# Graph attention with layer norm: one score tile in forty-eight goes from VectorE to ScalarE and GpSimd

## The chip, the cores and the metric

The kernel runs on one core of a Trainium2 chip. The metric is the device time of one execution in microseconds (us); times below are medians over runs on the chip. The core has five engines with a queue of instructions each: TensorE (PE in the profile; its weight loads stand apart as PEld), VectorE (DVE), ScalarE (ACT), GpSimd (POOL) and SyncE (SP, which here only issues transfers). An engine works its queue strictly in order; engines meet at semaphores, written by hand in this kernel.

## The reference

For each of 16 batches: 512 nodes with 384 features, 12 heads of 32 features, a boolean adjacency of 512 x 512 per batch.

```
h    = einsum('bnd,ade->bane', x, W);  th = tanh(h)
attn = (th @ w_src) + (th @ w_dst)^T;  attn = where(attn >= 0, attn, 0.2 * attn)
attn = softmax(where(adj, attn, -999))
o    = elu(attn @ h + b)                      # heads put side by side
gate = sigmoid(x @ H_w.T + H_b)
out  = layernorm(x + gate * o + (1 - gate) * x)
```

## The kernel before

The kernel has B = 16 steps, numbered b, each of which works on one batch and prepares the next. In a step the attention is done in HP = 6 pairs of heads, j = 0 to 5, each pair over C = 4 row blocks (c) of 128 nodes, so that a batch has 4 * H = 48 **score tiles** `ew` of 128 x 512 fp32 in the order t = 8j + 2c + k. The exponential of a leaky ReLU of a sum is split into factors, so that a tile is max(v, u) * adj: `v_all` is a row vector of the head, spread over all partitions by a transfer through memory; `u` is a scalar per partition; `ADJ` is the adjacency, turned into words that lie in PSUM (banks `adj01` and `adj23`). VectorE makes a tile in one instruction (`edges`, L820), TensorE multiplies it with `vals` (`attend`, L1082, two passes per tile), ScalarE copies the result out (`copy_out`, L525), TensorE turns it back (`transpose_out`, L1090) and VectorE divides by the sum (`attended`, L829 and L834). `ew` has SLOTS = 16 buffers; `ew_ready` counts the tiles made and `ew_free` those consumed.

Every order is written out by hand and is the same in each of the steps b = 1 to 13. What the prediction's steps touch:

- ScalarE (`step`): the copy of head pair 3, `gates(b, 2)` (L480), four row sums (L560), `gates(b, 3)`, four splits of x for batch b + 2 (L463), four small `out_bias` copies (L515), two row squares (L567), the adjacency words of blocks 0 and 1 of the next batch (`adjacency`, L505), `copy_out` 4, two more squares, adjacency blocks 2 and 3, `copy_out` 5; then step b + 1 begins with `features`, the tanh of the next batch's first block (L471).
- GpSimd: `weigh` (L296, then the half sums L302) for the four blocks, a bias transfer, `subtract_x` and `mix` (L339, L344, L347), `add_rows`, `values` (L333), `mean`, `split_low` (L307), a transfer, `variance` and `scale` (L355 to L364).
- VectorE: 48 tiles and between them, at fixed places, the rest: in j = 0 the divisions of the batch before, after the first tile of j = 1 the first `head_sums` (L782, waits for GpSimd's half sums), and so on until `scores_max` (L786) behind the last tile of j = 2. At tiles 0 and 4 of j = 0 it waits for two and four adjacency copies (`adj_done`).
- TensorE: features of the next batch (L982), heads 0 and 1, gates 0 and 1, `max_T` (L1014, waits for `scores_max`), heads 2 and 3, gates 2 and 3, heads 4 and 5, and the next features.

Of the kernel before, what the change touches and what calls it, by code (L numbers as in the profile page):

```python
# [6 lines left out]
BF16 = mybir.dt.bfloat16  # L7
# [3 lines left out]
ALU = mybir.AluOpType  # L11
# [3 lines left out]
P = 128  # L15
# [6 lines left out]
def gat_layernorm(nc, x, xT, adjT, W, HwT, w_rows, bias, H_b, out):  # L22
# [22 lines left out]
    VSLOTS = 3  # L45
    VB = 32
    assert N == 512 and H * E == D and B % 2 == 0

    ctx = ExitStack()
    with ctx:  # L50
# [6 lines left out]
        def sem(name):  # L57
# [6 lines left out]
        x_in = sb("x_in", [P, C, D])  # L64
        adj_in = sb("adj_in", [P, C, N], U8)

        w_hi = sb("w_hi", [P, KD, 2 * D], F32R)
# [32 lines left out]
        v_all = sb("v_all", [P, VSLOTS, 2, N])  # L100
        u = sb("u", [P, 2, C, H])
        vals = sb("vals", [P, 2, C, H, VW])
        gate_tanh = sb("gate_tanh", [P, C, D])
# [47 lines left out]
            scores mxT_done mxb_done exps_done v_turned vals_done  # L151
            ew_ready ew_free outT_copied tr_done inv_done att_done
            out_bias_done x_forms_done gate1_done elu_exp_done elu_done mixed moments sums_done mean_done squares_done var_done rstd_done y_done ld_x_last rest_last_done exp_last_done elu_last_done y_early_done elu_late_done y_late_done stats_done last_y_done""".split()
# [39 lines left out]
        def _(sp):  # L193
# [33 lines left out]
            def step(b, q, first, last, ahead=True):  # L227
# [11 lines left out]
                for j in range(VSLOTS, HP):  # L239
                    sp.wait_ge(S["ew_ready"], 4 * H * b + 2 * C * (j - 2))  # L240
                    load_v(b, q, j)
# [7 lines left out]
                if not last:  # L249
                    store_v(b + 1, 1 - q)  # L250
                    sp.wait_ge(S["st_v"], 64 * b + 128)
                    for j in range(VSLOTS):
                        if j:
                            sp.wait_ge(S["ew_ready"], 4 * H * b + 2 * C * (j + 4))
                        load_v(b + 1, 1 - q, j)
# [11 lines left out]
        def _(pool):  # L267
# [57 lines left out]
            def values(b, q):  # L325
# [3 lines left out]
                for c in range(C):  # L329
                    if isinstance(b, int) and b == 0:  # L330
# [3 lines left out]
                                    o[:, :, E:E + 1].broadcast_to([P, H, E]), ALU.mult).then_inc(S["vals_done"], 1)  # L334

            def subtract_x(b):
                pool.wait_ge(S["elu_done"], b + 1)
                pool.wait_ge(S["x_forms_done"], b + 1)
                g.tensor_tensor(ex[:], ex[:], x_plus1[:], ALU.subtract).then_inc(S["mixed"], 1)  # L339
# [26 lines left out]
            def step_last(b, q):  # L366
# [6 lines left out]
                pool.wait_ge(S["rest_last_done"], 1)  # L373
                g.tensor_tensor(rest_last[:], x_last, rest_last[:], ALU.subtract).then_inc(S["rest_last_done"], 1)
                y = y_last[:, :, EARLY]
                pool.wait_ge(S["exp_last_done"], 3)
# [9 lines left out]
            def step(b, q, first, last, ahead=True):  # L386
# [14 lines left out]
                if not last:  # L401
                    add_rows(b + 1, 1 - q)
                    values(b + 1, 1 - q)
                if not first:
                    mean(b - 1)
# [22 lines left out]
        def _(act):  # L428
            a = nc.scalar

            def before():
# [9 lines left out]
                for c in range(C):  # L441
                    adjacency(0, c)
                act.wait_ge(S["dve_setup"], DVE_SETUP)
                exps(0, 0)
# [43 lines left out]
            def exps(b, q):  # L488
# [10 lines left out]
                a.activation(vals[:, q, :, :, E], s_pos[:], ACT.Copy, scale=LIFT).then_inc(S["exps_done"], 1)  # L499

            def adjacency(b, c):
                act.wait_ge(S["ld_adj"], 16 * b + 16)
                if not isinstance(b, int) or b:
                    act.wait_ge(S["ew_ready"], 4 * H * b - 2 * C + 4 * (c // 2) + 4)
                a.activation(ADJ_WORDS[c // 2][:, c % 2], adj_in[:, c].bitcast(U16), ACT.Copy).then_inc(S["adj_done"], 1)  # L505

            def out_biases(b, q):
# [72 lines left out]
            def step(b, q, first, last, ahead=True):  # L580
# [24 lines left out]
                copy_out(b, q, 3)  # L605
                gates(b, 2)
                row_sums(b - 1)
                gates(b, 3)
# [7 lines left out]
                copy_out(b, q, 4)  # L616
                row_squares(b - 1, 2, C)
                for c in range(2, C):
                    adjacency(b + 1, c)
                copy_out(b, q, 5)  # L620

            def step_first(b, q):
# [11 lines left out]
                copy_out(b, q, 3)  # L634
                gates(b, 3)
                for c in range(C):
                    split(b + 2, q, c)
                copy_out(b, q, 4)
                for c in range(2):
                    adjacency(b + 1, c)  # L640
                out_biases(b + 1, 1 - q)
                for c in range(2, C):
                    adjacency(b + 1, c)
                copy_out(b, q, 5)

            def step_last(b, q):
# [13 lines left out]
                row_sums(b - 1)  # L660
                copy_out(b, q, 3)
                exp_early(q)
                copy_out(b, q, 4)
# [40 lines left out]
        def _(dve):  # L704
# [98 lines left out]
            def edges(b, q, j, between):  # L803

                for i in range(2 * C + 1):
                    for f in between.get(i, ()):
                        f()
                    if i == 2 * C:
                        break
                    c, k = i // 2, i % 2  # L810
                    h = 2 * j + k
# [130 lines left out]
        def _(pe):  # L942
# [125 lines left out]
            def attend(b, q, j):  # L1068
# [5 lines left out]
                for c in range(C):  # L1074
                    if j == 0 and isinstance(b, int) and b == 0:
                        pe.wait_ge(S["vals_done"], c + 1)
                    for k in range(2):
                        h = 2 * j + k
                        t = 2 * C * j + 2 * c + k

                        pe.wait_ge(S["ew_ready"], 4 * H * b + t + 1)
                        te.matmul(OUT[j % 2][VW * k:VW * k + VW, :], vals[:, q, c, h, :], ew[:, t % SLOTS, :],  # L1082
                                  start=(c == 0), stop=(c == C - 1)).then_inc(S["ew_free"], 1)
# [128 lines left out]
```

## Time and profile before

| | |
|---|---|
| time, median of 3 runs | 658.76 us (658.52 to 658.85) |
| the profiled execution | 658.69 us, its span 656.9 us |
| TensorE busy | 630.9 us (96%) |
| VectorE busy | 639.0 us (97%) |
| ScalarE busy | 429.6 us (65%) |
| GpSimd busy | 571.4 us (87%) |
| score tiles on VectorE | 768, 522.7 us together, mean 727 ns |
| chain that ended last | TensorE 48%, VectorE 30%, GpSimd 7%, ScalarE 2% |

The mean of one instruction is longer than the distance from one to the next, since neighbours on an engine overlap a little: 768 tiles of 727 ns would be 558 us, and take 522.7 us.

### The profile page before, as it was taken

The page shows a single profiled execution, that of the slowest core. Times are in us where ns is not written, and L with a number is a line of the kernel's source. Part 1 is how long each engine was busy: PE and PEld are TensorE (multiplying, and loading weights), DVE is VectorE, ACT ScalarE, POOL GpSimd, SP SyncE. Part 2 cuts the span into 40 slices and gives each one's busy share as a digit, 9 for nine tenths or more (in the row PEclk, how much of TensorE's full clock was granted, in tenths as well). Part 3 has the DMA queues.
Part 4 walks back from the last instruction along what each step waited for, and adds up shares of the span by engine and source line. Part 5 has one row for each costly group of instructions (what it writes and reads, how often), then busy time and mean ns, then how long its engine had stood idle before and what let it go on. Part 6 is the DMA issues. An engine that isn't in the chain of part 4 may idle for free.

```text
span 656.9 us, 12491 instructions
## 1 busy us (share of the span) xinstructions
PE 630.9 (96%) x3279; PEld 373.0 (57%) x3279; DVE 639.0 (97%) x1174; ACT 429.6 (65%) x936; POOL 571.4 (87%) x448
## 2 busy tenths in 40 slices
PE   8999999999999999999999999999999999999983
PEld 5565656574565647556664665656456565745531
DVE  7999999999999999999999999999999999999996
ACT  5434658486784848768485775848578584866664
POOL 2576998989989998998989999898999989997293
PEclk9999999999999999999999999999999999999997
DMA  6356549578475856848586584857747585675602
GB/s 209 118 131 181 178 123 274 128 196 248 140 235 129 235 164 176 240 146 251 133 210 190 154 238 144 249 132 200 228 142 233 139 259 126 187 211 131 217 40 97
DMA packets 54747, 117.62 MB, mean 179 GB/s; under 512 B 7106, under 2 KB 32452, under 8 KB 54724
## 3 DMA queue, kind: packets, MB, share of 16 engines
q1 hardware_dynamic: 42196, 81.56, 38.5%
q0 software_dynamic: 4320, 23.59, 19.2%
q10 hardware_dynamic: 8208, 12.19, 4.9%
q8 instruction: 11, 0.18, 0.1%
q14 instruction: 12, 0.10, 0.0%
HBM read 104.35 MB, written 12.98 MB: 179 GB/s over the span
## 4 chain that ended last, share of the span: by engine, by line
PE 48%; DVE 30%; issue 8%; POOL 7%; DMA 2%; ACT 2%; DVEq 1%; SPq 0%; POOLq 0%; ACTq 0%
PE out_T L1082 30%; DVE ew L820 20%; PE hg L982 13%; POOL th_w L296 4%; DVE sd L782 4%; DVE ex L842 3%; PE tr L1090 2%; POOL th_w L302 2%; PE hg L1047 1%; ACT th L471 1%; DMA xT_in<-in_xT 1%; DVE att L834 1%; DVEq L819 1%; PE hg L1014 1%; PE hg L1018 1%
## 5 line engine op out<-in xcount | busy, mean ns | idle before, releaser
L820 DVE SCALAR_TENSOR_TENSOR ew<-v_all,u,adj 128x512 f32<-128x512 f32 x768 | 522.7, 727 | 1.9 <-DMA v_all<-v_rows 1.2
L1082 PE MATMUL out_T<-ew,vals 128*64 128x512 f32 x1536 | 346.9, 597 | 0.0
L1082 PEld LDWEIGHTS out_T<-ew,vals 128*64 128x64 f32 x1536 | 106.3, 136 | 188.8 <-issue 144.1
L525 ACT ACTIVATE att_T<-out_T,out_bias 128x512 f32<-128x512 f32 x96 | 65.9, 686 | 116.1 <-PE out_T L1082 115.6
L296 POOL TENSOR_TENSOR th_w<-th,score_w 128x768 f32<-128x768 f32 x60 | 110.6, 1844 | 24.3 <-ACT th L471 24.3
L982 PE MATMUL hg<-w_hi,xT_hi 128*128 128x384 f32 x384 | 96.9, 360 | 0.8 <-ACT xT_hi L463 0.8
L982 PE MATMUL hg<-w_lo,xT_hi 128*128 128x384 f32 x384 | 88.2, 337 | 0.0
L982 PE MATMUL hg<-w_hi,xT_lo 128*128 128x384 f32 x384 | 87.7, 336 | 0.0
L302 POOL TENSOR_TENSOR th_w<-th_w 128x384 f32<-128x384 f32 x60 | 82.6, 1376 | 4.7
L982 PEld LDWEIGHTS hg<-w_hi,xT_hi 128*128 128x128 f32 x384 | 62.6, 189 | 40.2 <-issue 39.4
L982 PEld LDWEIGHTS hg<-w_lo,xT_hi 128*128 128x128 f32 x384 | 69.1, 188 | 0.0
L982 PEld LDWEIGHTS hg<-w_hi,xT_lo 128*128 128x128 f32 x384 | 68.9, 188 | 0.0
L333 POOL TENSOR_TENSOR vals<-h_sb,vals 128x384 f32<-128x384 f32 x64 | 53.3, 866 | 16.2 <-ACT vals L499 16.2
L339 POOL TENSOR_TENSOR ex<-ex,x_plus 128x1536 f32<-128x1536 f32 x15 | 56.4, 3758 | 11.4 <-ACT x_plus L530 11.4
L307 POOL TENSOR_TENSOR xT_lo<-xT_in,xT_hi 128x384 fp32r<-128x384 f32 x60 | 58.6, 1014 | 0.5 <-ACT xT_hi L463 0.5
L1090 PE MATMUL tr<-ident,att_T 128*128 128x128 f32 x384 | 53.1, 273 | 4.8 <-ACT att_T L525 4.8
L347 POOL TENSOR_TENSOR y<-x_in,ex 128x1536 f32<-128x1536 f32 x15 | 52.1, 3470 | 2.2 <-POOL ex L344 2.0
L344 POOL TENSOR_TENSOR ex<-gate,ex 128x1536 f32<-128x1536 f32 x15 | 52.0, 3467 | 1.4
L480 ACT ACTIVATE gate_tanh<-hg 128x384 f32<-128x384 f32 x60 | 29.5, 492 | 34.1 <-PE hg L982 32.8
L1090 PEld LDWEIGHTS tr<-ident,att_T 128*128 128x128 f32 x384 | 45.6, 141 | 10.8 <-ACT att_T L525 8.7
L471 ACT ACTIVATE th<-hg 128x384 f32<-128x384 f32 x64 | 31.7, 495 | 29.6 <-PE hg L982 29.6
L782 DVE TENSOR_REDUCE sd<-th_w 128x24 f32<-128x384 f32 (+1 forms) x64 | 36.5, 570 | 3.9 <-POOL th_w L302 3.7
(116 smaller groups left out, 669.0 us busy)
## 6 DMA issues: line engine op xcount, KB each, us to landing
v_all<-v_rows SPq DMA_DIRECT2D x95, 512.0 KB, 4.6
xT_in<-in_xT SPq DMA_DIRECT2D x16, 768.0 KB, 9.5
h_sb<-in_bias POOLq DMA_DIRECT2D x15, 768.0 KB, 6.7
x_in<-in_x SPq DMA_DIRECT2D x15, 768.0 KB, 4.6
gate_tanh<-in_H_b POOLq DMA_DIRECT2D x15, 768.0 KB, 9.4
out<-y ACTq DMA_DIRECT2D x15, 768.0 KB, 3.7
adj_in<-in_adjT SPq DMA_DIRECT2D x16, 256.0 KB, 9.8
v_rows<-v_turn SPq DMA_DIRECT2D x64, 6.0 KB
```

Of the source, the lines that this page charges most:

```text
L296: g.tensor_tensor(th_w[:, c % 2], th[:, c].unsqueeze(1).broadcast_to([P, 2, D]), score_w[:], ALU.mult).then_inc(S["thw_done"], 1)
L302: g.tensor_tensor(t[:, :, 0:E // 2], t[:, :, 0:E // 2], t[:, :, E // 2:E], ALU.add).then_inc(S["thh_done"], 1)
L307: g.tensor_tensor(xT_lo[:, q, :, n], xT_in[:, :, n], xT_hi[:, q, :, n].bitcast(F32), ALU.subtract).then_inc(S["xlo_done"], 1)
L333: g.tensor_tensor(o[:, :, 0:E], h_sb[:, c].rearrange("p (h e) -> p h e", e=E), o[:, :, E:E + 1].broadcast_to([P, H, E]), ALU.mult).then_in ...
L339: g.tensor_tensor(ex[:], ex[:], x_plus1[:], ALU.subtract).then_inc(S["mixed"], 1)
L347: g.tensor_tensor(y[:], x_in[:], ex[:], ALU.add).then_inc(S["mixed"], 1)
L525: a.activation(att_T[:, j % 2], OUT[j % 2][:], ACT.Identity, bias=out_bias[:, q, j:j + 1]).then_inc(S["outT_copied"], 1)
L782: ve.tensor_reduce(sd_ckh[:, 2 * H * c:2 * H * (c + 1)], t, AX.X, ALU.add).then_inc(S["sd_done"], 1)
L820: ve.scalar_tensor_tensor(out=twos(ew[:, (2 * C * j + i) % SLOTS, :]), in0=twos(v_all[:, j % VSLOTS, k]), scalar=u[:, q, c, h:h + 1], in1= ...
L982: last = te.matmul(o, l, r, start=(i == 0), stop=(i == len(mms) - 1))
L1082: te.matmul(OUT[j % 2][VW * k:VW * k + VW, :], vals[:, q, c, h, :], ew[:, t % SLOTS, :], start=(c == 0), stop=(c == C - 1)).then_inc(S["ew ...
L1090: last = te.transpose(TR[j % 2][:, c * P:(c + 1) * P], att_T[:, j % 2, c * P:(c + 1) * P], ident[:])
```

## The change

The last tile of each batch, t = 47 (head 11, row block 3), is no longer made by VectorE. ScalarE makes max(v, u) in two passes, relu(v - u) and then + u, after a small instruction that negates `u`; GpSimd multiplies the result with `adj_side`, a bf16 copy of the adjacency's last row block that ScalarE makes once per batch from `adj_in`. `ew_ready` counts 47 tiles per batch (EW), TensorE waits for `side_ready` ahead of tile 47, and the third `v_all` load of the next batch also waits for ScalarE's passes.

```diff
+    SIDE = 1
+    EW = 4 * H - SIDE
+        adj_side = sb("adj_side", [P, N], BF16)
+        minus_u = sb("minus_u", [P, SIDE])
...
 SyncE
-                            sp.wait_ge(S["ew_ready"], 4 * H * b + 2 * C * (j + 4))
+                            sp.wait_ge(S["ew_ready"], EW * b + min(2 * C * (j + 4), EW))
+                        if j == VSLOTS - 1:
+                            sp.wait_ge(S["side_scored"], 2 * SIDE * b + 2 * SIDE)
                         load_v(b + 1, 1 - q, j)
...
 GpSimd
+            def side_tiles(b):
+                pool.wait_ge(S["adj_side_done"], b + 1)
+                pool.wait_ge(S["side_scored"], 2 * SIDE * b + 2 * SIDE)
+                tiles = ew[:, SLOTS - SIDE:SLOTS, :]
+                g.tensor_tensor(tiles, tiles, adj_side[:].unsqueeze(1).broadcast_to([P, SIDE, N]), ALU.mult).then_inc(S["side_ready"], 1)
...
                     values(b + 1, 1 - q)
+                side_tiles(b)
                 if not first:
                     mean(b - 1)
...
 ScalarE
+            def side_tiles(b, q):
+                act.wait_ge(S["side_ready"], b)
+                for i in range(SIDE):
+                    h = H - SIDE + i
+                    a.activation(minus_u[:, i:i + 1], u[:, q, C - 1, h:h + 1], ACT.Copy, scale=-1.0).then_inc(S["side_u"], 1)
+                act.wait_ge(ld_v[2], 32 * b + 32)
+                act.wait_ge(S["ew_free"], 4 * H * b + 4 * H)
+                act.wait_ge(S["side_u"], SIDE * b + SIDE)
+                for i in range(SIDE):
+                    k = 2 - SIDE + i
+                    a.activation(ew[:, SLOTS - SIDE + i, :], v_all[:, 2, k], ACT.Relu, bias=minus_u[:, i:i + 1]).then_inc(S["side_scored"], 1)
+                for i in range(SIDE):
+                    h = H - SIDE + i
+                    act.wait_ge(S["side_scored"], 2 * SIDE * b + i + 1)
+                    a.activation(ew[:, SLOTS - SIDE + i, :], ew[:, SLOTS - SIDE + i, :], ACT.Identity,
+                                 bias=u[:, q, C - 1, h:h + 1]).then_inc(S["side_scored"], 1)
...
-                    act.wait_ge(S["ew_ready"], 4 * H * b - 2 * C + 4 * (c // 2) + 4)
+                    act.wait_ge(S["ew_ready"], EW * b + (0 if c // 2 else SIDE - C))
...
+            def adjacency_side(b):
+                if not isinstance(b, int) or b:
+                    act.wait_ge(S["side_ready"], b)
+                a.activation(adj_side[:], adj_in[:, C - 1], ACT.Copy).then_inc(S["adj_side_done"], 1)
...
                 gates(b, 2)
+                side_tiles(b, q)
                 row_sums(b - 1)
...
                 row_squares(b - 1, 2, C)
+                adjacency_side(b + 1)
                 for c in range(2, C):
                     adjacency(b + 1, c)
...
 VectorE
+                    if 2 * C * j + i >= EW:
+                        continue
...
 TensorE
-                        pe.wait_ge(S["ew_ready"], 4 * H * b + t + 1)
+                        if t < EW:
+                            pe.wait_ge(S["ew_ready"], EW * b + t + 1)
+                        elif t == EW:
+                            pe.wait_ge(S["side_ready"], b + 1)
```

In step b = 0 `side_tiles` stands behind `gates(b, 3)`, in the last step behind `copy_out` 3, and GpSimd's in the last step behind the second `rest_last`.

ScalarE's queue in a middle step, from the gate copy of block 2 to the row sums. Before:

```order
L480 ACTIVATE gate_tanh<-hg 128x384
L554 REGISTER_ALU
L556 REGISTER_ALU
L560 ACTIVATE scratch,sums<-y 128x384 x2
L559 REGISTER_ALU
L560 ACTIVATE scratch,sums<-y 128x384
```

Of the change, where three instructions (a 128x1 negation and two passes over a tile) stand ahead of the row sums:

```order
L495 ACTIVATE gate_tanh<-hg 128x384
L520 ACTIVATE minus_u<-u 128x1
L521 ISA
L526 ACTIVATE ew<-v_all,minus_u 128x512
L529 ISA
L530 ACTIVATE ew<-ew,u 128x512
L591 REGISTER_ALU
L593 REGISTER_ALU
L597 ACTIVATE scratch,sums<-y 128x384 x2
```

So all that follows in this queue, the four adjacency copies too, stands behind three instructions more.

The same queue from the first adjacency copies to the next step's first tanh. Before:

```order
L505 ACTIVATE adj<-adj_in 128x256 x2
L519 REGISTER_ALU
L522 REGISTER_ALU
L525 ACTIVATE att_T<-out_T,out_bias 128x512
L567 ACTIVATE scratch,squares<-y,neg_mean 128x384 x2
L505 ACTIVATE adj<-adj_in 128x256 x2
L519 REGISTER_ALU
L522 REGISTER_ALU
L525 ACTIVATE att_T<-out_T,out_bias 128x512
L466 ISA
L471 ACTIVATE th<-hg 128x384
```

Of the change:

```order
L537 ACTIVATE adj<-adj_in 128x256 x2
L556 REGISTER_ALU
L559 REGISTER_ALU
L562 ACTIVATE att_T<-out_T,out_bias 128x512
L604 ACTIVATE scratch,squares<-y,neg_mean 128x384 x2
L542 ACTIVATE adj_side<-adj_in 128x512
L537 ACTIVATE adj<-adj_in 128x256 x2
L556 REGISTER_ALU
L559 REGISTER_ALU
L562 ACTIVATE att_T<-out_T,out_bias 128x512
L481 ISA
L486 ACTIVATE th<-hg 128x384
```

The copy of `adj_side` stands ahead of the adjacency blocks 2 and 3 and so also ahead of `copy_out` 5 and the tanh.

GpSimd's queue between `values` and `split_low` of a middle step, of the change:

```order
L339 TENSOR_TENSOR vals<-h_sb,vals 128x12x32 x4
L344 ISA
L346 TENSOR_TENSOR ew<-ew,adj_side 128x512
L362 ISA
L363 TENSOR_TENSOR neg_mean<-sums,minus_share 128x4
```

The multiply stands between what were neighbours; it is the one instruction that this queue gains.

## Rows read from the trace of the kernel before

**Rows 1.** Windows, six turns from 195 to 428 us: busy us of each engine

```profile
sum 233.00, PE 229.53 PEld 137.28 DVE 230.85 ACT 160.48 POOL 220.19; mean PE 38.26 PEld 22.88 DVE 38.47 ACT 26.75 POOL 36.70
```
**Rows 2.** Chain in order of time, 273 to 352 us: start us, us, what

```profile
277.20 0.33 PE hg L1014
...
315.94 0.33 PE hg L1014
...
328.54 7.02 PE out_T L1082 x32
335.55 1.80 PE hg L982 x9
...
338.12 1.86 POOL th_w L296
...
340.06 1.03 POOL th_w L302
...
341.11 0.05 DVE sd L782
```
**Rows 3.** Timeline of VectorE, 311 to 350 us: start us, us, what [idle before]

```profile
328.57 9.37 DVE L820 SCALAR_TENSOR_TENSOR ew<-v_all,u,adj 128x512 f32<-128x512 f32 x14
...
341.11 0.55 DVE L782 TENSOR_REDUCE sd<-th_w 128x24 f32<-128x384 f32 x1 [0.40 <-POOL th_w L302]
...
342.90 1.75 DVE L842 SCALAR_TENSOR_TENSOR ex<-ex,att 128x1536 f32<-128x1536 f32 x1
```
**Rows 4.** Timeline of ScalarE, 311 to 352 us

```profile
332.01 0.67 ACT L505 ACTIVATE adj<-adj_in 128x256 int32<-128x256 uint16 x2
...
334.49 0.67 ACT L505 ACTIVATE adj<-adj_in 128x256 int32<-128x256 uint16 x2
335.70 0.69 ACT L525 ACTIVATE att_T<-out_T,out_bias 128x512 f32<-128x512 f32 x1 [0.54 <-PE out_T L1082]
337.47 0.49 ACT L471 ACTIVATE th<-hg 128x384 f32<-128x384 f32 x1 [1.07 <-PE hg L982]
```
**Rows 5.** Window of one stretch: busy us (x instructions) by engine, clock, DMA, GB/s

```profile
325.95:335.70 9.75, 9.75 (x53) 4.93 (x51) 9.75 (x18) 9.09 (x31) 9.59 (x14) 1.00 0.67 203
```
**Rows 6.** Timeline of GpSimd, 311 to 352 us

```profile
330.12 0.22 POOL L351 TENSOR_TENSOR neg_mean<-sums,minus_share 128x4 f32<-128x4 f32 x1
...
336.64 0.20 POOL L364 TENSOR_TENSOR shift<-neg_mean,rstd 128x4 f32<-128x4 f32 x1
338.12 1.86 POOL L296 TENSOR_TENSOR th_w<-th,score_w 128x768 f32<-128x768 f32 x1 [1.28 <-ACT th L471]
...
342.98 2.54 POOL L302 TENSOR_TENSOR th_w<-th_w 128x384 f32<-128x384 f32 x1
```
**Rows 7.** Groups by line and form: busy us, mean ns of one | idle before

```profile
L525 ACT ACTIVATE att_T<-out_T,out_bias 128x512 f32<-128x512 f32 x96 | 65.9, 686 | 116.1 <-PE out_T L1082 115.6
...
L307 POOL TENSOR_TENSOR xT_lo<-xT_in,xT_hi 128x384 fp32r<-128x384 f32 x60 | 58.6, 1014 | 0.5 <-ACT xT_hi L463 0.5
...
L567 ACT ACTIVATE scratch<-y,neg_mean 128x384 f32<-128x384 f32 x60 | 36.2, 605 | 1.3 <-POOL neg_mean L351 1.0
...
L463 ACT ACTIVATE xT_hi<-xT_in 128x384 fp32r<-128x384 f32 x64 | 28.1, 513 | 0.8 <-DMA xT_in<-in_xT 0.8
L319 POOL TENSOR_TENSOR hb_sum<-h_sb 128x768 f32<-128x768 f32 x15 | 27.7, 1847 | 4.7 <-DMA h_sb<-in_bias 4.7
...
L495 ACT ACTIVATE u<-d_rel 128x48 f32<-128x48 f32 x16 | 3.6, 227 | 0.0
```
**Rows 8.** Timeline of GpSimd in step b = 0

```profile
68.09 1.02 POOL L302 TENSOR_TENSOR th_w<-th_w 128x384 f32<-128x384 f32 x1
```
**Rows 9.** Timeline of VectorE in step b = 0

```profile
69.30 0.53 DVE L782 TENSOR_REDUCE sd<-th_w 128x24 f32<-128x384 f32 x1
```
**Rows 10.** Timeline of VectorE in the last step, its first and last tiles

```profile
605.72 4.04 DVE L820 SCALAR_TENSOR_TENSOR ew<-v_all,u,adj 128x512 f32<-128x512 f32 x6 [0.20 <-DMA v_all<-v_rows]
...
643.91 0.69 DVE L896 SCALAR_TENSOR_TENSOR ex<-ex,att 128x512 f32<-128x512 f32 x1 [0.21 <-ACT ex L686]
```

More of the change, by code:

```diff
@@ L151, in gat_layernorm @@
             scores mxT_done mxb_done exps_done v_turned vals_done
-            ew_ready ew_free outT_copied tr_done inv_done att_done
+            ew_ready ew_free adj_side_done side_u side_scored side_ready outT_copied tr_done inv_done att_done
             out_bias_done x_forms_done gate1_done elu_exp_done elu_done mixed moments sums_done mean_done squares_done var_done rstd_done y_done ld_x_last rest_last_done exp_last_done elu_last_done y_early_done elu_late_done y_late_done stats_done last_y_done""".split()
@@ L239, in step @@
                 for j in range(VSLOTS, HP):
-                    sp.wait_ge(S["ew_ready"], 4 * H * b + 2 * C * (j - 2))
+                    sp.wait_ge(S["ew_ready"], EW * b + 2 * C * (j - 2))
                     load_v(b, q, j)
@@ L403, in step @@
                     values(b + 1, 1 - q)
+                side_tiles(b)
                 if not first:
@@ L442, in before @@
                     adjacency(0, c)
+                adjacency_side(0)
                 act.wait_ge(S["dve_setup"], DVE_SETUP)
@@ L635, in step_first @@
                 gates(b, 3)
+                side_tiles(b, q)
                 for c in range(C):
@@ L641, in step_first @@
                 out_biases(b + 1, 1 - q)
+                adjacency_side(b + 1)
                 for c in range(2, C):
@@ L661, in step_last @@
                 copy_out(b, q, 3)
+                side_tiles(b, q)
                 exp_early(q)
```

## The prediction

> **What bounds the kernel now.** The table of busy shares comes first and settles nothing: in six turns of the middle (233 us) VectorE is busy for 230.85 us and TensorE for 229.53 us [rows 1]. Both look full, so the question is which of them waits for what, and the chain in order of time answers it. It repeats with a period of 38.74 us, from one `max_T` (277.20) to the next (315.94) [rows 2]. In one turn it runs:
>
> 1. TensorE from `max_T` at 315.94 through heads 2 to 5 and the gates to the end of the next batch's first features, 335.55 + 1.80 = 337.35 [rows 2]: 21.4 us without a gap.
> 2. ScalarE's tanh of these features at 337.47 [rows 4], GpSimd's product at 338.12 and its half sums, 340.06 to 341.09 [rows 2]: 3.8 us.
> 3. VectorE's first `head_sums` at 341.11 [rows 2], then everything in its queue up to `scores_max`, for which the next `max_T` waits: the remaining 13.6 us (38.74 - 25.17).
>
> The reader is to see what part 3 does not hold. Tile 47 stands ahead of it. VectorE's 14 tiles from 328.57 are eight of j = 5 and six of the next j = 0, one every 0.663 us ((9.37 - 0.07) / 14, the last one's tail taken off) [rows 3]; so tile 47 is made from 333.2 to 333.87, and at 341.11 VectorE has already stood 0.40 us for GpSimd's half sums [rows 3]. This small wait is the place that decides: the tile taken out lies on the side of it that is early.
>
> **What the change removes.** 0.66 us of VectorE per batch, ahead of that wait. In the middle of the kernel the 0.40 us would only become 1.06 us: worth nothing. The next batch's `v_all` transfer also comes just in time there; at the first tile of the last step VectorE waits 0.20 us for it [rows 10], so the tile gone there is worth nothing either. In step b = 0 VectorE runs without waits, and its first `head_sums` at 69.30 follows half sums that end at 68.09 + 1.02 = 69.11 [rows 8, 9]: worth 0.2 us once. At the end the tile stands ahead of an instruction that waits 0.21 us for ScalarE's exponential [rows 10]: nothing.
>
> **What it adds on ScalarE, first block.** At 325.95, behind the gate copy, come the negation and two passes. No row is 512 wide with SBUF on both sides; the nearest are `copy_out` with 686 ns (512 wide, but from PSUM) and the squares with 605 ns (SBUF and the same kind of bias, but 384 wide) [rows 7]. The squares' 605 and the 0.08 us from them to `copy_out` say that a pass is at least 0.69; I take a little more, 0.71 us, because SBUF is read. The negation is a small instruction like the `u` exponential, 0.23 us [rows 7]. Each waits for the one before it, so neighbours do not overlap, except the last by 0.1 us: 0.23 + 0.71 + 0.71 + 0.1 for three hand-overs - 0.1 = **1.65 us**. Bounds: 0.605 a pass, as if the width cost nothing, gives 1.4; the squares widened in proportion, 605 x 512 / 384 = 0.81, and hand-overs twice as long give 2.0.
>
> The Trainium skill ("ScalarE: Activation LUTs", What ACT_TABLE_LOAD costs) gives 280 ns + 0.833 ns per element with a pointer bias, 186 ns without, and an overlap of about 93 ns between neighbours. For these three that is 0.19 + 0.71 + 0.71 - 0.09 = 1.5 us, an estimate; 605 ns at 384 wide [rows 7] fits it (600). By it each turn would lose 0.15 us less than by my sum, 2 us in all.
>
> **Second block.** The `adj_side` copy, 512 wide without a pointer bias, has 513 ns at 384 wide beside it [rows 7]: 0.62 us, and 0.52 us as a distance to the next. Bounds 0.33 (a word copy, 0.67 for two [rows 4]) and 0.7.
>
> Is there room for 2.17 us? From 325.95 to 335.70 ScalarE is busy for 9.09 of 9.75 us [rows 5], nearly all of the rest being the 0.54 us before `copy_out` 5, and before the tanh it has 1.07 us more [rows 4]. With the 0.1 us of overlap that each idle stretch also cost, the room is 1.8 us. What is late next, path by path:
>
> - *The tanh*: 2.17 - 1.8 = 0.37 us late. `copy_out` 5 ends near 337.9, and TensorE's second transpose after the features waits some 0.4 us for it. The wait is hidden: TensorE is idle for 233 - 229.53 = 3.47 us in six turns [rows 1], 0.58 a turn, and part 1 of the chain has none of it, so it lies where the late transpose is.
> - *The adjacency copies, for VectorE's j = 0*: the first two end at 332.68 + 1.65 = 334.33, so tile 0 starts at 334.40 where VectorE could have started at 333.2. The next two end at 335.16 + 2.17 = 337.33 [rows 4], so tile 4 starts at 337.40 and not at 333.87 + 4 x 0.663 = 336.52: 0.88 us late. Less the wait of 0.40 us [rows 3] that it eats, `head_sums` is **0.48 us** late.
> - *GpSimd*: it gains one multiply. 384 wide costs 1014 ns and 768 wide 1847 ns [rows 7]; on the line between, 512 wide is 1.29 us, 1.25 as a distance. It starts where `mean` did, at 330.12 [rows 6], when ScalarE's passes (done by 327.7) are there, and TensorE needs tile 47 only at 335.1 (it is the last of 16 tiles in the 7.02 us from 328.54 [rows 2]). What follows in the queue, ending with `shift` at 336.84 [rows 6], is late by 1.25 us, or by ScalarE's 1.65 us where it waits for the squares: 338.49 at most, against `weigh` at 338.12 [rows 6]. That is 0.37 us at most, no more than the tanh brings anyway.
>
> The rule that speaks against the multiply is in the Trainium skill ("GPSIMD Engine Reference", 8. Key points): the engine shares its SBUF interfaces with VectorE and contends with VectorE instructions with two SBUF inputs. The trace agrees where it applies: a half sum of 1.02 us [rows 8] takes 2.54 us at 342.98 [rows 6], beside the elu at 342.90 [rows 3], whose two inputs lie in SBUF. The multiply would run beside score tiles, whose adjacency comes from PSUM, so I leave it at 1.25 us.
>
> **The sum.** The three paths meet at the same `head_sums`, so they do not add: the latest counts, 0.48 us. It returns in each turn that ends in a `weigh`, the steps b = 1 to 13 (behind b = 14 no `weigh` follows). 13 x 0.48 - 0.2 = +6.0 us. The profiled execution is 658.69 us for a span of 656.9, 0.07 us from the median of 658.76, so the forecast is **664.8 us**.
>
> **Rivals.**
> - *VectorE's work sets the period, and the wait is an accident of one turn* (faster). For it: the busy share, and the Trainium skill's advice ("Perfetto Trace Analysis", Optimizing Scalar/DVE Operations) to move work to ScalarE or GpSimd when VectorE is saturated. Every turn would then shorten by up to 0.66 us, but TensorE has only 0.58 us a turn [rows 1]: 13 x 0.58 = 7.5, so 651 us. It decides only if GpSimd's half sums come at least 0.4 us earlier than now; nothing in the change moves them forward. 10%.
> - *All is absorbed* (no change). If the passes and the copy take 1.7 us and not 2.17, tanh and `copy_out` fit into the room, and the adjacency path loses 0.1 us or nothing: 657.5 to 660, say 658.6. For it: every margin is under 0.5 us. Against it: even 1.4 + 0.33 leaves tile 4 at 336.89 + 0.07, 0.44 late against 0.40. 14%.
> - *GpSimd becomes the limit.* From a multiply of 1.6 us on, `weigh` is later than the 0.48 us; at 2.0 us it is 0.88 us a turn, 670 us; if it is stretched like the half sum (by 1.5 us), 1.6 us a turn and about 680. 10%.
>
> **How the numbers follow.** The forecast's own case is 0.3 to 0.8 us a turn, 662.5 to 669 us: 60%; a smaller loss between it and "absorbed" has 6%. The range of 658.3 to 670 takes in the small losses and most of the absorbed case and of the slow multiply, and leaves out the faster case, a quarter of the absorbed one and the stretched multiply, some 18%. Within 0.2% (1.3 us) is about what a measurement of this kernel tells from no change: faster 0.10, same 0.14, slower 0.76.
>
> **What would show it.** In a middle turn: a period of 39.2 to 39.3 us; VectorE idle for over 1 us ahead of its first j = 0 tile, released by ScalarE's adjacency copy, and again ahead of tile 4; the wait at `head_sums` small or gone; no idle time of ScalarE between the gate copy and the tanh; passes of 0.71 us and a multiply of 1.29 us. The prediction is wrong if the period is unchanged with the `head_sums` wait grown to 1 us (absorbed), if GpSimd stands without idle time ahead of `weigh` (its rival), or if the period is shorter, which would mean that VectorE's work before the wait counted after all.

## The result, and the profile after

The change makes the kernel slower: **665.78 us** (median of 4 runs, 665.71 to 666.15) against 658.73 us, a ratio of 1.0109 with a 95% interval of 1.0091 to 1.0126. The forecast was 664.8 us in a range of 658.3 to 670.0.

The page of the profile after, its lines for the span, the busy times, the chain that ended last and the costliest group:

```profile
span 663.9 us, 12596 instructions
PE 631.8 (95%) x3279; PEld 372.0 (56%) x3279; DVE 629.8 (95%) x1158; ACT 459.3 (69%) x1000; POOL 590.5 (89%) x464
PE 34%; DVE 31%; issue 15%; ACT 12%; POOL 4%; DMA 2%; DVEq 1%; ACTq 1%; SPq 0%; POOLq 0%
L864 DVE SCALAR_TENSOR_TENSOR ew<-v_all,u,adj 128x512 f32<-128x512 f32 x752 | 514.2, 729 | 20.8 <-ACT adj L537 18.7
```

The work of VectorE went down from 639.0 to 629.8 us and the span up by 7.0 us. The last number names the place: VectorE stands 18.7 us ahead of tiles, for ScalarE's adjacency copies. ScalarE's share of the last chain went from 2% to 12%.

**Where the 7.0 us lie.** `max_T` divides the span. Timelines of TensorE around its first and last periodic `max_T`, before (L1014):

```profile
82.95 0.33 PE L1014 MATMUL hg<-ident,d_max_c 128*128 128x128 f32 x1 [0.56 <-DVE d_max_c L786]
...
587.55 0.33 PE L1014 MATMUL hg<-ident,d_max_c 128*128 128x128 f32 x1 [0.41 <-DVE d_max_c L786]
```

and after (L1058):

```profile
82.54 0.33 PE L1058 MATMUL hg<-ident,d_max_c 128*128 128x128 f32 x1 [0.43 <-DVE d_max_c L828]
...
593.72 0.33 PE L1058 MATMUL hg<-ident,d_max_c 128*128 128x128 f32 x1 [0.54 <-DVE d_max_c L828]
```

Up to the first: -0.41 us. The 13 turns between them: 511.18 against 504.60, **+6.58 us, 0.506 a turn**. From the last to the span's end: 663.9 - 593.72 = 70.18 against 69.35, **+0.83 us** (the span is printed to 0.1 us, so this part is known to within 0.1). Together 7.0. Of the -0.41 us, 0.15 lie ahead of the very first `max_T` of the kernel, at 18.07 us against 18.22, where the profiled executions of all versions differ by up to 0.5 us; the rest, 0.25 us, lies around the end of step b = 0.

**One turn.** Chain in order of time of after, 270 to 362 us (start, us, what):

```profile
279.21 0.32 PE hg L1058
...
318.49 0.33 PE hg L1058
...
357.87 0.32 PE hg L1058
```

The turns take 39.28 and 39.38 us. [Rows 2] show a turn of 38.74; the turns alternate there, and the one that begins at 315.94 takes 38.91. Inside one, VectorE's timeline (315 to 362 us) from the first tiles of the next j = 0 on:

```profile
331.12 4.68 DVE L864 SCALAR_TENSOR_TENSOR ew<-v_all,u,adj 128x512 f32<-128x512 f32 x7
337.14 2.72 DVE L864 SCALAR_TENSOR_TENSOR ew<-v_all,u,adj 128x512 f32<-128x512 f32 x4 [1.34 <-ACT adj L537]
340.03 1.41 DVE L864 SCALAR_TENSOR_TENSOR ew<-v_all,u,adj 128x512 f32<-128x512 f32 x2 [0.16 <-ACT adj L537]
...
344.13 0.54 DVE L824 TENSOR_REDUCE sd<-th_w 128x24 f32<-128x384 f32 x1
```

In [rows 3] 14 tiles ran here without a gap, and `head_sums` waited 0.40 us. Now seven tiles of j = 5 end at 335.80, VectorE waits 1.34 us for adjacency blocks 0 and 1 and 0.16 us for blocks 2 and 3, and `head_sums` waits for nothing. Counted from `max_T` it starts at 344.13 - 318.49 = 25.64 us, against 25.17. This 0.47 us is the loss of the turn, 39.38 against 38.91. In the turns between, `head_sums` came at 25.07 us before and comes at 25.62 now, a loss of 0.55.

ScalarE's timeline, 327 to 342 us, shows why the copies are late:

```profile
328.14 0.49 ACT L495 ACTIVATE gate_tanh<-hg 128x384 f32<-128x384 f32 x1 [0.99 <-PE hg L1026]
328.52 0.20 ACT L520 ACTIVATE minus_u<-u 128x1 f32<-128x1 f32 x1
328.83 0.72 ACT L526 ACTIVATE ew<-v_all,minus_u 128x512 f32<-128x512 f32 x1
329.59 0.72 ACT L530 ACTIVATE ew<-ew,u 128x512 f32<-128x512 f32 x1
330.22 0.51 ACT L597 ACTIVATE scratch<-y 128x384 f32<-128x384 f32 x1
...
336.23 0.67 ACT L537 ACTIVATE adj<-adj_in 128x256 int32<-128x256 uint16 x2
...
338.71 0.61 ACT L542 ACTIVATE adj_side<-adj_in 128x512 bf16<-128x512 uint8 x1
339.23 0.67 ACT L537 ACTIVATE adj<-adj_in 128x256 int32<-128x256 uint16 x2
339.85 0.67 ACT L562 ACTIVATE att_T<-out_T,out_bias 128x512 f32<-128x512 f32 x1
340.42 0.47 ACT L486 ACTIVATE th<-hg 128x384 f32<-128x384 f32 x1
```

The negation and the two passes hold the queue from 328.52 to 330.22, `adj_side` from 338.71 to 339.23. The two idle stretches of [rows 4], 0.54 us ahead of `copy_out` 5 and 1.07 us ahead of the tanh, are gone: the queue is full up to the tanh.

GpSimd's timeline, 330 to 350 us:

```profile
332.64 1.18 POOL L346 TENSOR_TENSOR ew<-ew,adj_side 128x512 f32<-128x512 f32 x1
...
340.57 0.20 POOL L376 TENSOR_TENSOR shift<-neg_mean,rstd 128x4 f32<-128x4 f32 x1
341.10 1.85 POOL L302 TENSOR_TENSOR th_w<-th,score_w 128x768 f32<-128x768 f32 x1 [0.33 <-ACT th L486]
343.03 1.02 POOL L308 TENSOR_TENSOR th_w<-th_w 128x384 f32<-128x384 f32 x1
```

`weigh` still waits 0.33 us for the tanh, so GpSimd's own queue doesn't delay it. It starts 22.61 us behind `max_T`, against 22.18 [rows 2, 6], and its half sums end at 344.05, 0.08 us ahead of `head_sums`. VectorE's own queue and the path through tanh and GpSimd are thus late by nearly the same amount.

The lines by form of what the change adds (busy us, mean ns of one):

```profile
L526 ACT ACTIVATE ew<-v_all,minus_u 128x512 f32<-128x512 f32 x16 | 11.6, 726 | 1.8
L530 ACT ACTIVATE ew<-ew,u 128x512 f32<-128x512 f32 x16 | 11.6, 725 | 0.5
L542 ACT ACTIVATE adj_side<-adj_in 128x512 bf16<-128x512 uint8 x16 | 9.9, 618 | 0.0
L520 ACT ACTIVATE minus_u<-u 128x1 f32<-128x1 f32 x16 | 3.1, 195 | 0.0
L346 POOL TENSOR_TENSOR ew<-ew,adj_side 128x512 f32<-128x512 f32 x16 | 18.7, 1168 | 1.8 <-ACT ew L530 1.8
```

### The profile page after: what moved, and what is told of

It reads as the page before. It is cut to its first block, busy times and chain, and to the rows that moved or that the text cites. A ratio compares the mean times of both kernels' runs of the same rounds, so it can differ in the third digit from the quotient of the medians.

```text
span 663.9 us, 12596 instructions
## 1 busy us (share of the span) xinstructions
PE 631.8 (95%) x3279; PEld 372.0 (56%) x3279; DVE 629.8 (95%) x1158; ACT 459.3 (69%) x1000; POOL 590.5 (89%) x464
## 4 chain that ended last, share of the span: by engine, by line
PE 34%; DVE 31%; issue 15%; ACT 12%; POOL 4%; DMA 2%; DVEq 1%; ACTq 1%; SPq 0%; POOLq 0%
PE out_T L1129 22%; DVE ew L864 19%; PE hg L1026 8%; DVE sd L824 4%; DVE ex L886 3%; ACT scratch L604 2%; ACT adj L537 2%; ACT xT_hi L478 2%; DVE att L878 2%; ACT scratch L597 2%; PE tr L1137 1%; POOL th_w L302 1%; DVEq L863 1%; ACT ew L526 1%; DMA xT_in<-in_xT 1%
## 5 line engine op out<-in xcount | busy, mean ns | idle before, releaser
L864 DVE SCALAR_TENSOR_TENSOR ew<-v_all,u,adj 128x512 f32<-128x512 f32 x752 | 514.2, 729 | 20.8 <-ACT adj L537 18.7
L1137 PE MATMUL tr<-ident,att_T 128*128 128x128 f32 x384 | 55.9, 275 | 8.0 <-ACT att_T L562 8.0
L878 DVE TENSOR_TENSOR att<-tr,rden 128x256 f32<-128x256 f32 x96 | 39.5, 412 | 0.0
```

What stands on the lines that cost most here:

```text
L864: ve.scalar_tensor_tensor(out=twos(ew[:, (2 * C * j + i) % SLOTS, :]), in0=twos(v_all[:, j % VSLOTS, k]), scalar=u[:, q, c, h:h + 1], in1= ...
L878: ve.tensor_tensor(o, t[:, :, :, 0:E], rden[:, j % 2].unsqueeze(3).broadcast_to([P, C, 2, E]), ALU.mult).then_inc(S["att_done"], 1)
L1137: last = te.transpose(TR[j % 2][:, c * P:(c + 1) * P], att_T[:, j % 2, c * P:(c + 1) * P], ident[:])
```

## The experiments

**Theories.** *Queue*: ScalarE's added work, where it stands, makes the adjacency copies late; the tile taken from VectorE is worth nothing. *Rivals*: GpSimd's multiply costs the time; or the tile is worth something and ScalarE costs more than the 0.5 us a turn. The table has times in us; "turns" are the 13 between the first and the last periodic `max_T`, "tail" the rest of the span behind the last. Each ratio is taken against executions of the kernel before that ran beside it (medians 658.73 to 658.76 down to side_copy_last, 658.58 down to side_early_sums_later, 658.46 for the last four), and is not the quotient of the medians. "Turns" and "tail" are of one profiled execution; two of these are not typical. In tile_dropped it took 659.63 us and in sums_later 658.22, 0.6 and 1.3 us over their medians, and in both the first of the 13 turns is long (39.86 and 39.89 us, 38.92 before), with an elu of 2.27 and 2.51 us in it. The other twelve have a mean of 38.82 us in tile_dropped, 38.69 in sums_later and 38.81 before.

| kernel | time | ratio to before (95%) | turns | tail |
|---|---|---|---|---|
| before | 658.73 | 1 | 504.60 | 69.35 |
| after | 665.78 | 1.0109 (1.0091 to 1.0126) | 511.18 | 70.18 |
| tile_dropped | 659.07 | 1.0001 (0.9991 to 1.0011) | 505.66 | 69.49 |
| passes_only | 665.13 | 1.0090 (1.0073 to 1.0107) | 511.10 | 69.54 |
| no_multiply | 665.68 | 1.0099 (1.0082 to 1.0116) | 510.99 | 70.29 |
| side_copy_last | 664.93 | 1.0087 (1.0070 to 1.0104) | 510.28 | 70.31 |
| last_by_vector | 664.89 | 1.0094 (1.0077 to 1.0111) | 511.09 | 69.41 |
| side_early | 660.17 | 1.0023 (1.0013 to 1.0032) | 505.60 | 70.20 |
| sums_later | 656.89 | 0.9976 (0.9966 to 0.9986) | 504.12 | 69.34 |
| side_early_sums_later | 658.58 | 1.0003 (0.9991 to 1.0015) | 503.77 | 70.25 |
| elu_later | 662.59 | 1.0059 (1.0046 to 1.0073) | 508.31 | 69.24 |
| tile_dropped_elu_later | 662.56 | 1.0060 (1.0047 to 1.0074) | 508.49 | 69.41 |
| side_early_elu_later | 663.58 | 1.0076 (1.0062 to 1.0090) | 508.69 | 70.26 |
| best | 662.85 | 1.0069 (1.0055 to 1.0083) | 508.58 | 69.59 |

### tile_dropped: the tile goes, nothing comes

Of the kernel before, with tile 47 left out: the last score tile isn't computed, and TensorE multiplies what the buffer holds.

```diff
                     if 2 * C * j + i >= EW:
                         continue
...
-                        pe.wait_ge(S["ew_ready"], 4 * H * b + t + 1)
+                        if t < EW:
+                            pe.wait_ge(S["ew_ready"], EW * b + t + 1)
```

> VectorE makes 47 tiles per batch and nobody makes the last one: no passes on ScalarE, no copy of the last row block, no multiply; TensorE multiplies what lies in the buffer, so the last head's sum is left wrong in one row block. If the tile removed lies on the early side of the wait for GpSimd's half sums, the time is that of the kernel before less 0.2 to 0.4 us of step b = 0: 658.3 us, and VectorE's wait at the first head_sums grows from 0.4 to 1 us. If VectorE's work sets the period: 649 to 652 us.

No difference: 1.0001. The tile was worth nothing where it stood. Its waits (who waits for whom: us, times, longest) show what took its place, VectorE standing for `v_all`, for TensorE's transposes, and still for GpSimd, where before the three were 1.2 us in 4, 2.1 in 3 and 3.7 in 12:

```profile
DVE ew L848 <- DMA v_all<-v_rows: 5.4, 12, 0.9
DVE rden L857 <- PE tr L1119: 5.0, 12, 1.3
...
DVE sd L808 <- POOL th_w L306: 4.2, 14, 0.4
```

The expected growth of the wait at `head_sums` to 1 us did not come: its longest is still 0.4 us. The freed time is waited away earlier in the turn.

### passes_only: ScalarE's work comes, the tile stays

The kernel before with ScalarE's negation, two passes and copy at their places in the change, in steps 0 to 14; the last step stays as before. All 48 tiles stay on VectorE, nothing reads the passes' result, and ScalarE's unused `scratch` output is bf16 to make space.

```diff
+                side_passes(b, q)
                 row_sums(b - 1)
...
+                adjacency_side(b + 1)
                 for c in range(2, C):
                     adjacency(b + 1, c)
```

> The kernel before, VectorE keeps all 48 tiles; ScalarE makes the negation, the two passes and the adj_side copy at the places of the change, into tiles that nobody reads; no GpSimd multiply (the row sums' unread output is narrower to make room). If ScalarE's queue alone makes the loss: 13 turns x 0.5 = +6.5, 665.2 us, although VectorE does more work than in the change. If the GpSimd multiply makes it: 658.7 us. If it takes both together: between 660 and 663.

The turns lose 6.50 of the 6.58 us with nothing but ScalarE's part, and the tail, whose step has none of it, stays at 69.54. VectorE's timeline shows the same wait, shorter by the tile that now fills it:

```profile
337.32 2.72 DVE L842 SCALAR_TENSOR_TENSOR ew<-v_all,u,adj 128x512 f32<-128x512 f32 x4 [0.67 <-ACT adj L523]
340.20 1.41 DVE L842 SCALAR_TENSOR_TENSOR ew<-v_all,u,adj 128x512 f32<-128x512 f32 x2 [0.16 <-ACT adj L523]
```

1.34 us of wait without the tile, 0.67 with it: the tile's 0.66 us only changed into wait.

### no_multiply: GpSimd's part goes

The change without GpSimd's multiply: tile 47 goes unmasked to TensorE, which waits for ScalarE's second pass.

```diff
-                side_tiles(b)          # GpSimd, middle and last step
...
-                            pe.wait_ge(S["side_ready"], b + 1)
+                            pe.wait_ge(S["side_scored"], 2 * b + 2)
```

> The change without GpSimd's multiply: TensorE takes the tile from ScalarE unmasked. If ScalarE's queue is the limit: 665.5 us, as the change, and GpSimd idle about 1.2 us more ahead of its variance. If the multiply is: 659 to 661 us.

The turns stay at 510.99. The multiply changed into a wait for ScalarE's squares, 16.2 us in 14 where the change has 7.6:

```profile
POOL var L361 <- ACT scratch L593: 16.2, 14, 3.3
```

GpSimd is not the limit in the turns. The tail stays long too, 70.29 us, though the multiply is gone from the last step as well.

### side_copy_last: the second block behind all adjacency copies

```diff
-                adjacency_side(b + 1)
                 for c in range(2, C):
                     adjacency(b + 1, c)
+                adjacency_side(b + 1)
```

The copy is counted in `adj_done` here, and GpSimd's multiply waits for that.

> The change with the adj_side copy behind the adjacency copies of blocks 2 and 3 instead of ahead of them. VectorE's tile 4 then starts about 0.35 us earlier, but the copy still stands ahead of the tanh, which in the trace of the change is 0.46 us later behind its features than before. If the two paths are as close as that trace shows: 0.04 to 0.1 us a turn gained, 664.7 to 665.4 us, with VectorE's wait at head_sums back. If only the adjacency path counts: 13 x 0.4 gained, about 660.5 us.

The second wait, ahead of tile 4, is gone, the first is unchanged:

```profile
336.82 4.04 DVE L864 SCALAR_TENSOR_TENSOR ew<-v_all,u,adj 128x512 f32<-128x512 f32 x6 [1.36 <-ACT adj L537]
```

But the turns gain 0.90 us, 0.07 each. VectorE comes earlier to `head_sums` and there meets the other path (in every second turn of the middle it stands 0.1 us for GpSimd): the tanh is where it was, with `adj_side` still ahead of it. Mending one of two paths that are late together is worth their difference.

### last_by_vector: the last batch as before

Steps 0 to 14 as in the change; in the last step VectorE makes all 48 tiles.

```diff
-                side_tiles(b)          # GpSimd, last step
-                side_tiles(b, q)       # ScalarE, last step
...
-                    if 2 * C * j + i >= EW:
+                    if 2 * C * j + i >= EW and not (isinstance(b, int) and b == B - 1):
```

> The change, but in the last batch VectorE makes all 48 tiles and neither ScalarE nor GpSimd has a part in it. In the trace of the change VectorE's elu at the end takes 1.52 us instead of 0.69, beside a GpSimd addition that runs 6 us later than it did, and the time behind the last max_T is 0.8 us longer. If the passes ahead of ScalarE's early exponential cause that: 0.8 us less than the change, 665.0 us, with the elu at 0.69 us. If not: 665.8 us.

The tail goes from 70.18 to 69.41 and the time by 0.9 us; the turns stay. The term is real. The end of the change, timelines of VectorE and then of GpSimd:

```profile
650.00 1.52 DVE L940 SCALAR_TENSOR_TENSOR ex<-ex,att 128x512 f32<-128x512 f32 x1 [0.86 <-ACT ex L728]
...
645.28 1.82 POOL L390 TENSOR_TENSOR ex<-ex,gate_tanh 128x768 f32<-128x768 f32 x1 [1.30 <-ACT ex L724]
...
649.16 1.81 POOL L395 TENSOR_TENSOR ex<-ex,x_plus 128x768 f32<-128x768 f32 x1
```

and of last_by_vector:

```profile
649.92 0.69 DVE L938 SCALAR_TENSOR_TENSOR ex<-ex,att 128x512 f32<-128x512 f32 x1 [0.21 <-ACT ex L726]
...
647.40 1.83 POOL L394 TENSOR_TENSOR ex<-ex,x_plus 128x768 f32<-128x768 f32 x1
```

VectorE's elu of 128 x 512, 0.69 us long in [rows 10] as here, takes 1.52 us in the change: it was issued at 650.00, while GpSimd's addition ran until 650.97, and ended 0.55 us after that.

last_by_vector takes out the passes and the multiply together; no_multiply tells which of them moved the addition. The same timelines of no_multiply:

```profile
649.89 1.51 DVE L929 SCALAR_TENSOR_TENSOR ex<-ex,att 128x512 f32<-128x512 f32 x1 [0.87 <-ACT ex L717]
...
645.17 1.82 POOL L383 TENSOR_TENSOR ex<-ex,gate_tanh 128x768 f32<-128x768 f32 x1 [2.45 <-ACT ex L713]
```

Without the multiply the elu is as long, 1.51 us. It is ScalarE's part: in the last step the negation and the passes stand behind `copy_out` 3, directly ahead of the early exponential, which starts at 644.36 in the change and at 642.59 in last_by_vector, 1.77 us apart. GpSimd waits for it ahead of its product, with the multiply long done (at 643.99), and all that follows on GpSimd is late by the same 1.77 us.

### side_early: the same work at other places

The passes stand behind the exponentials, ahead of `copy_out` 3, with a buffer `side` of their own; the `adj_side` copy stands behind all adjacency blocks. ScalarE's `scratch` is one byte wide to make space; its row squares take 605 ns as before, and 606 with the two bytes of passes_only.

```diff
                 exps(b + 1, 1 - q)
+                side_tiles(b, q)
                 copy_out(b, q, 3)
                 gates(b, 2)
-                side_tiles(b, q)
```

> The change with a buffer of its own for the tile, so that the passes can stand behind the exponentials and ahead of copy_out 3, where ScalarE idles for 1.2 us, and with the adj_side copy behind the adjacency copies (the row sums' unread output is narrower to make room). Nothing but 0.52 us is left in the crowded stretch, which has 1.8 us of room. If place and not work makes the loss: 658.7 - 0.3 + 0.8 (the end of the last step stays as in the change) = 659.2 us, 658.5 to 660. If the work itself does, on ScalarE or GpSimd: 664 to 666 us.

505.60 us for the turns: with the same added work, 5.58 of the 6.58 us are back. ScalarE's timeline shows the passes in what was idle time, and the idle time ahead of the tanh again:

```profile
322.87 0.72 ACT L527 ACTIVATE side<-v_all,minus_u 128x512 f32<-128x512 f32 x1
...
337.47 0.50 ACT L487 ACTIVATE th<-hg 128x384 f32<-128x384 f32 x1 [0.52 <-PE hg L1027]
```

So the place makes the loss, not the amount. And the tile still brings nothing: VectorE waits for GpSimd at `head_sums` again (4.9 us in 13, 3.7 in 12 before) and for `v_all` (4.6 us in 8, 1.2 in 4 before). What makes the turns 1.0 us longer than before was not tested.

### sums_later, side_early_sums_later: move the wait itself

If the wait at `head_sums` hides the tile, `head_sums` one tile later should uncover it.

```diff
-                        put(5 if first else 1, lambda: head_sums(b + 1, 0))
+                        put(5 if first else 2, lambda: head_sums(b + 1, 0))
```

> The kernel before with nothing of the change; only the first head_sums stands one tile later in VectorE's queue, so that VectorE makes a tile during the 0.4 us in which it waited for GpSimd's half sums. If that wait closes the loop: 13 x 0.35 gained, 654.2 us. If it is an accident without effect: 658.7 us.

> side_early and the later head_sums together. If the tile taken off VectorE is worth something once VectorE no longer waits, the period is then set by TensorE (38.3 to 38.4 us): 13 x 0.45 gained, + 0.5: 653.4 us, up to 1 us under sums_later. If GpSimd, which is then busy for over 98% of a turn, sets it: 655 to 658 us.

Both fall short. sums_later gains 0.24% (656.89 us, 654.2 expected), and is the fastest version found; with side_early the tile adds nothing to that: 658.58 us is 1.7 more, 0.9 of it in the tail. The table shows 0.35 us less for the turns only because of the long first turn of sums_later; the other twelve have a mean of 38.73 us against 38.69. The wait is gone: six turns of sums_later by windows (195 to 428 us) have VectorE busy for 232.69 of 233 us, against 230.85 [rows 1].

```profile
sum 233.00, PE 230.35 PEld 137.72 DVE 232.69 ACT 160.68 POOL 220.15; mean PE 230.35 PEld 137.72 DVE 232.69 ACT 160.68 POOL 220.15
```

But part of the busy time is new. The elu takes 2.10 us here, and 1.75 us in [rows 3]. Timelines of VectorE and GpSimd:

```profile
342.80 2.10 DVE L842 SCALAR_TENSOR_TENSOR ex<-ex,att 128x1536 f32<-128x1536 f32 x1
...
341.43 1.85 POOL L296 TENSOR_TENSOR th_w<-th,score_w 128x768 f32<-128x768 f32 x1
343.36 2.40 POOL L302 TENSOR_TENSOR th_w<-th_w 128x384 f32<-128x384 f32 x1
```

The product ends at 343.28, and the elu 1.62 us after it. The half sum that comes next takes 2.40 instead of 1.02 us, but that is not new: beside the elu of the kernel before it took 2.54 [rows 6]. New is that VectorE stands too. In most of the turns after the first the elu takes 2.00 and 2.10 us by turns, so it takes back 0.25 and 0.35 us of a wait of 0.30 and 0.40. What is left, 0.05 us, and the overlap of about 0.07 us that an idle stretch costs (a tile of 727 ns every 663) make 0.12, the measured gain of a turn; this sum is an estimate.

### The elu one place further

The cure I tried was to move the elu clear of the product, in four versions: sums_later with it (elu_later), the same with tile 47 left out as in tile_dropped (tile_dropped_elu_later), side_early with both moves, and best, which adds to that last_by_vector's last step and the first `v_all` transfer ahead of the x load.

```diff
-                        put(3, lambda: elu(b - 1, 1 - q))
+                        put(4, lambda: elu(b - 1, 1 - q))
```

> sums_later gained 0.13 us a turn and not 0.35: its elu, which now meets a GpSimd product of 1.86 us, takes 2.0 us instead of 1.75. Here the elu also stands one tile later, behind the end of that product. If the two engines shut each other out there: the elu back at 1.75 us, VectorE without waits at 38.5 us a turn, 13 x 0.33 gained, 654.4 us. If the elu is long for another reason: as sums_later, 656.9 us.

> The same two moves, and nobody makes the last tile of a batch (the last head's sum is left wrong in one row block): what the tile is worth when no wait of VectorE absorbs it and its replacement costs nothing. If VectorE's work sets the period of elu_later, the tile brings up to 0.66 us a turn, cut off by TensorE at 38.3 us: 652 us. If something else already sets it: as elu_later, within 0.5 us.

> side_early with the same two moves: the change at a place where ScalarE has room, on a kernel in which VectorE does not wait. If the tile is worth anything there: 0.3 to 1.5 us under elu_later plus 0.8 us for the end of the last step, 653.9 to 655 us. If v_all's transfer, for which side_early_sums_later waited in 10 batches, takes the tile's gain: 655 to 657 us.

> side_early_elu_later, with the last batch left to VectorE and with v_all's chain of transfers ahead of the load of x, which waits for GpSimd: v_all lands 0.5 us earlier. If v_all is what is late: 1.5 us or more under side_early_elu_later, 652.5 us, and VectorE's waits for the transfer gone. If TensorE is the limit: only the 0.8 us of the last step.

The direction was wrong in all four: 5.7 to 6.7 us more than sums_later. Lines by form, the elu of elu_later:

```profile
L842 DVE SCALAR_TENSOR_TENSOR ex<-ex,att 128x1536 f32<-128x1536 f32 x15 | 35.2, 2346 | 0.0
```

The mean was 1749 ns before and is 2008 in sums_later. From the third turn on the elu takes 2.42 and 2.52 us by turns, 0.42 more than in sums_later, and the turns take 39.20 and 39.02 us against 38.79 and 38.60: 0.41 us more, 5.4 us in 13 turns, of the 5.7 measured. (The table's difference, 4.19 us, has the long first turn of sums_later in it.) Timelines of VectorE and GpSimd in elu_later:

```profile
345.13 2.52 DVE L842 SCALAR_TENSOR_TENSOR ex<-ex,att 128x1536 f32<-128x1536 f32 x1
...
345.03 1.00 POOL L302 TENSOR_TENSOR th_w<-th_w 128x384 f32<-128x384 f32 x1
346.00 3.35 POOL L296 TENSOR_TENSOR th_w<-th,score_w 128x768 f32<-128x768 f32 x1
```

The elu now falls at the start of a half sum, ends 1.62 us after that is done (346.03), and the next product takes 3.35 instead of 1.85 us. GpSimd pays 1.50 us here and 1.52 in the kernel before (2.54 for 1.02); what grew is VectorE's part. Leaving the tile out changes nothing here either (508.49 against 508.31). VectorE's timeline of tile_dropped_elu_later has a wait behind the place of the missing tile, where elu_later has none:

```profile
339.58 0.21 DVE L857 RECIPROCAL rden<-tr 128x8 f32<-128x8 f32 x1 [0.60 <-PE tr L1119]
```

So VectorE stands for TensorE's transposes (7.6 us in 14, 2.1 in 3 in elu_later), and its elu then lasts 2.53 us beside the same half sum. Which of the two, the transposes or the elu's tie to GpSimd, would hide the tile alone was not tested. best shows that the transfer isn't the reason (turns 508.58 against 508.69) and gains 0.7 us in the tail.

## Why the prediction was right

1. **"The small wait decides; the tile is worth nothing in the middle"**: the value is right, tile_dropped gave 1.0001 and side_early no gain. The reason is right only in part: the wait at `head_sums` did not grow to 1.06 us. Without the tile VectorE stands for `v_all` and for TensorE's transposes ahead of it, and 0.4 us are left at `head_sums`.
2. **The first block, 1.65 us**: measured 1.70 (328.52 to 330.22), the passes 726 and 725 ns for 0.71 us. The two dependent passes start 0.76 us apart (328.83 and 329.59), so they do not overlap. The Trainium skill ("ScalarE: Activation LUTs", What ACT_TABLE_LOAD costs) gives 280 + 0.833 x 512 = 706 ns for one pass, an estimate; the trace's 726 ns are 3% more.
3. **The second block, 0.62 and 0.52 us**: 618 ns and 0.52 us.
4. **The adjacency path, +0.48 us a turn**: +0.506 in the turns. VectorE waits at exactly the two places named. Tile 4 starts 21.54 us behind `max_T`; forecast was 337.40 - 315.94 = 21.46. The 0.48 came from one turn. In every second turn the wait that the loss eats is 0.30 us and not 0.40, and there the loss is 0.55. The same haste made part 3 of the chain 13.6 us: 38.74 and 25.17 belong to different turns, and the one with 25.17 has 13.74.
5. **The tanh, +0.37 us**: `weigh` came 0.43 us later. It is hidden behind the adjacency path by only about 0.1 us, as side_copy_last showed.
6. **GpSimd, multiply 1.29 us, not the limit**: 1.17 us, and no_multiply changed nothing. Contention beside tiles whose adjacency comes from PSUM did not appear: the 16 take 1157 to 1183 ns, with a mean of 1168.
7. **Step b = 0, -0.2 us**: -0.41 up to the first periodic `max_T`, of which -0.25 around the end of that step and the rest before it.
8. **The end, costed at nothing**: wrong. This is the step that failed. I asked only whether VectorE's tile stood ahead of a wait, and put what ScalarE gains in the last step at nothing without a reason. The passes stand there ahead of the early exponential, make it 1.77 us late, and with it GpSimd's addition, which so comes to lie beside the elu. It measured +0.83 us, and last_by_vector gave 0.8 us of the tail back; the multiply has no part in it, as no_multiply shows.

6.0 forecast and 7.0 measured differ by this term (0.83), by the turns (0.33) and by b = 0 (-0.2). The forecast is close because of the adjacency path, which the trace shows as described; the path through the tanh would have given nearly the same time. The rivals "VectorE's work sets the period", "all is absorbed" and "GpSimd becomes the limit" fell with tile_dropped, passes_only and no_multiply.

## What to carry to other kernels

Ask of an engine that looks full where its last small wait stands: VectorE at 97% with one wait of 0.3 to 0.4 us a turn behind the tile gained nothing from 0.66 us less work per turn. Then ask of the engine that takes the work what stands behind the new instructions in its queue and who waits for that; here 2.2 us on an engine that is busy 65% of the time cost 0.5 us a turn at one place and 0.08 at another. Do this for the first and the last step by themselves, where the order is another. And when a move shifts two engines against each other, look at which of their instructions lie side by side afterwards, at the end of the kernel too.

## What the runs showed of the hardware

VectorE's elu, whose two inputs lie in SBUF, and a GpSimd instruction hardly share time: whichever comes second stands until the first is done. The elu of 128 x 1536 ended 1.61 to 1.62 us after the GpSimd instruction in the midst of which it was issued, in sums_later and in elu_later alike, whether it had been issued 0.48 or 0.90 us before that instruction's end (2.10 and 2.52 us long, 1.75 otherwise). The GpSimd instruction behind it was longer by 1.4 us (a half sum, 2.40 for 1.02) and 1.5 us (a product, 3.35 for 1.85). In the kernel before, GpSimd alone pays (2.54 for 1.02), as the elu is issued just when a product ends. At the end of the change the elu of 128 x 512 paid 0.83 us (0.69 to 1.52). The Trainium skill ("GPSIMD Engine Reference", 8. Key points) says that GpSimd contends for its SBUF interfaces with VectorE instructions that have two SBUF inputs. The trace agrees. In these runs the price depends on the moment: the same elu costs 1.75, 2.10 or 2.52 us, by how much of a GpSimd instruction is left when it is issued. What was not tried is an order in which the elu is issued just as a GpSimd instruction ends and GpSimd then waits for something else.
